# Transposes of the gated values, gate passes and convolution taps in other steps of a delta-rule attention loop

## What is computed

```python
qkvz = (x @ W_qkvz)                       # q, k, v, z
q, k, v = silu(causal 4-tap convolution of q, k, v)
def step(S, inp):                         # one token, one value head
    S = S * exp(g_t)
    delta = (v_t - k_t @ S) * beta_t
    S = S + outer(k_t, delta)
    return S, q_t @ S
gated = silu(z) * rms_norm(out) * norm_w
return gated @ W_out
```

## The kernel before, in words

| step | PE fill | ACT after copy | DVE after mask |
|---|---|---|---|
| 2 | inversion start g=1, last q passes | tanh v | conv K tap 3 |
| 3 | 7 Z0 | tap q | qk(0) |
| 4 | 7 Z0 | tanh k, gated(0) | qk(1) |
| 5 | 3 Z0, turn 0 | gated(1) | low(0) |
| 6 | 2 Z0, turn 1 | | low(1) |
| 7 | 5 Z0, product 0 | | add 0, conv Q tap 1 |
| 8 | product 1 | | add 1, conv Q tap 2 |
| 9 | product 2 | tanh q, tanh Z0 | add 2, conv Q tap 3 |
| 10 | product 3, 4 Z1 | | add 3 |
| 11 | 8 Z1 | | silu of Z0 |
| 12 | 4 Z1, transposes of k | squares of k | |
| 13 | 8 Z1 | | |

## Time and profile before

### The profile page before, as it was taken

How to read it: one execution, slowest core, us unless ns; L and a number is a source line. 1 busy time by engine, 2 the same in 40 slices (tenths; PEclk the granted TensorE clock), 3 DMA queues, 4 the chain that set the end, 5 groups by cost and what they waited for, 6 DMA issues and landing times. The chain is left out here.

```text
span 3966.3 us, 76921 instructions
## 1 busy us (share of the span) xinstructions
PE 3621.5 (91%) x29348; PEld 3031.0 (76%) x29348; DVE 2334.4 (59%) x4155; ACT 2062.8 (52%) x5168; POOL 2334.6 (59%) x2899
## 2 busy tenths in 40 slices
PE   5995699999999999999999999999999999997798
PEld 4884487878788878887878787878787888886587
DVE  4654466666666666666666666666666666663464
ACT  3432355555555555555555555555555555553243
POOL 2101567676767676767676767676766676763110
PEclk8997799999999999999999999999999999998899
DMA  4323100000000000000000000000000000000521
GB/s 159 104 32 69 50 23 23 22 24 23 24 22 23 23 23 23 23 22 23 23 24 22 24 22 23 23 24 23 23 23 23 22 23 23 22 26 24 176 54 33
DMA packets 142396, 140.47 MB, mean 35 GB/s; under 512 B 84176, under 2 KB 115152, under 8 KB 140880
## 3 DMA queue, kind: packets, MB, share of 16 engines
q1 hardware_dynamic: 136992, 120.16, 10.3%
q0 software_dynamic: 4464, 14.36, 1.0%
q10 hardware_dynamic: 576, 1.03, 0.1%
HBM read 109.11 MB, written 26.21 MB: 34 GB/s over the span
## 5 line engine op out<-in xcount | busy, mean ns | idle before, releaser
L1870 ACT ACTIVATE at_t<-at_inv 128x512 f16<-128x512 f32 x768 | 459.8, 599 | 591.9 <-PE at_inv L1679 591.9
L2054 DVE TENSOR_TENSOR at_pm<-at_prod,at_cst 128x512 f16<-128x512 f32 x768 | 529.4, 689 | 146.8 <-PE at_prod L1462 120.1
L1462 PE MATMUL at_proj<-x_hi,at_w_hi 128*128 128x512 f32 x1024 | 438.0, 428 | 15.6 <-POOL at_w_lo L2128 15.6
L1462 PE MATMUL at_proj<-x_lo,at_w_hi 128*128 128x512 f32 x1024 | 421.9, 412 | 0.0
L1462 PE MATMUL at_proj<-x_hi,at_w_lo 128*128 128x512 f32 x1024 | 416.5, 407 | 0.0
L1462 PE MATMUL at_prod<-at_t,at_nlhi 128*128 128x128 f16 x3584 | 367.6, 219 | 20.0 <-ACT at_t L1868 13.0
L2213 POOL TENSOR_TENSOR at_gt_lo<-at_cst,at_gates 128x512 fp32r<-128x512 f32 x256 | 262.1, 1045 | 115.2 <-PE at_misc L1462 115.1
L1462 PE MATMUL at_misc<-at_wo_hi,at_gt_hi 128*128 128x512 f32 x512 | 230.9, 451 | 94.5 <-DVE resid L2028 61.3
L1462 PE MATMUL at_proj<-at_w_hi,x_lo 128*128 128x256 f32 x1024 | 308.5, 301 | 0.0
L1462 PE MATMUL at_proj<-at_w_hi,x_hi 128*128 128x256 f32 x1024 | 297.9, 291 | 0.1
L1980 DVE SCALAR_TENSOR_TENSOR at_cv_v<-at_proj,at_cw,at_cv_v 128x511 f32<-128x511 f32 (+2 forms) x384 | 287.5, 749 | 16.3 <-ACT at_cv_v L1796 2.8
(11 more groups left out here) (291 smaller groups left out, 10829.0 us busy)
## 6 DMA issues: line engine op xcount, KB each, us to landing
at_gb<-decays SPq DMA_DIRECT2D x64, 512.0 KB, 3.6
at_e<-w_qkvz SPq DMA_DIRECT2D x32, 512.0 KB, 3.6
ffn_weights<-ffn_w SPq DMA_DIRECT2D x1, 11776.0 KB, 36.3
ffn_w<-ffn_weights POOLq DMA_DIRECT2D x4, 2688.0 KB, 23.8
at_gb<-w_qkvz SPq DMA_DIRECT2D x16, 512.0 KB, 3.6
at_gb<-w_out SPq DMA_DIRECT2D x16, 512.0 KB, 3.5
f_xnext<-x_in SPq DMA_DIRECT2D x4, 1024.0 KB, 5.3
f_xres<-x_res SPq DMA_DIRECT2D x4, 1024.0 KB, 5.3
```

The lines of the kernel that those rows point to most:

```text
L1462: return nc.tensor.matmul(out, lhsT, rhs, start=start, stop=stop)
L1870: own["a_t"].up(A(grown(t16[:, s % R].rearrange("p a t -> p (a t)"), s // R), grown(psT[s % R], s // R), ACT.Copy))
L2054: own["d_p"].up(V.tensor_tensor(pm[:, g].rearrange("p (c t) -> p c t", c=CH), psP[:].rearrange("p (c t) -> p c t", c=CH), mask.unsqueeze(1 ...
```

## The change

Gate passes are spread differently over the fill lists of steps 3 to 13, and those of steps 7 to 10 stand ahead of the output product of their step. Turn 0 moves from step 5 to step 4. On ACT, gated(0) moves from step 4 to step 3, tap q from 3 to 4, and tanh k from 4 to 6. On DVE, the qk products move up by one step, with a wait for ACT's squares added in front (L1872; they write the same tile), and taps 1 and 2 of q run in step 7 ahead of add 0, tap 3 in step 8 behind add 1. No arithmetic is added or taken away.

| step | PE fill | ACT after copy | DVE after mask |
|---|---|---|---|
| 2 | as before | as before | conv K tap 3, qk(0) |
| 3 | 5 Z0 | gated(0) | qk(1) |
| 4 | 5 Z0, turn 0 | tap q | |
| 5 | 5 Z0 | gated(1) | low(0) |
| 6 | turn 1, 2 Z0 | tanh k | low(1) |
| 7 | 4 Z0, product 0 | | conv Q taps 1 and 2, add 0 |
| 8 | 3 Z0, product 1 | | add 1, conv Q tap 3 |
| 9 | 4 Z1, product 2 | as before | add 2 |
| 10 | 4 Z1, product 3 | | add 3 |
| 11 | 6 Z1 | | as before |
| 12 | 3 Z1, transposes of k | as before | |
| 13 | 7 Z1 | | |

```diff
                 if has_delta:
-                    fill[3].append(gates_in(Z0_U, 0, 7))
-                    fill[4].append(gates_in(Z0_U, 7, 14))
-                    fill[5].append(gates_in(Z0_U, 14, 17))
-                    fill[6].append(gates_in(Z0_U, 17, 19))
-                    fill[7].append(gates_in(Z0_U, 19, 24))
+                    fill[3].append(gates_in(Z0_U, 0, 5))
+                    fill[4].append(gates_in(Z0_U, 5, 10))
+                    fill[5].append(gates_in(Z0_U, 10, 15))
                 if behind:
                     for h in range(R):
-                        fill[5 + h].append(lambda h=h: turn_gated(h, j - 1))
+                        fill[4 + 2 * h].append(lambda h=h: turn_gated(h, j - 1))
+                if has_delta:
+                    fill[6].append(gates_in(Z0_U, 15, 17))
+                    fill[7].append(gates_in(Z0_U, 17, 21))
+                    fill[8].append(gates_in(Z0_U, 21, 24))
+                    fill[9].append(gates_in(Z1_U, 0, 4))
+                    fill[10].append(gates_in(Z1_U, 4, 8))
+                if behind:
                     for c in range(WPROD):
                         fill[7 + c].append(lambda c=c: out_product(c, j - 1))
                 if has_delta:
-                    fill[10].append(gates_in(Z1_U, 0, 4))
-                    fill[11].append(gates_in(Z1_U, 4, 12))
-                    fill[12].append(gates_in(Z1_U, 12, 16))
-                    fill[13].append(gates_in(Z1_U, 16, 24))
+                    fill[11].append(gates_in(Z1_U, 8, 14))
+                    fill[12].append(gates_in(Z1_U, 14, 17))
+                    fill[13].append(gates_in(Z1_U, 17, 24))
...
-                if has_prep:
-                    steps[3].append(lambda: tap(Q_U))
-                    steps[4].append(lambda: tanh(K_U))
                 if behind:
                     for h in range(R):
-                        steps[4 + h].append(lambda h=h: gated(j - 1, h))
+                        steps[3 + 2 * h].append(lambda h=h: gated(j - 1, h))
+                if has_prep:
+                    steps[4].append(lambda: tap(Q_U))
+                    steps[6].append(lambda: tanh(K_U))
...
                 def qk(h):
                     wait(dve, "s_kq", j + 1)
+                    wait(dve, "a_sqo", R * j)
...
-                        steps[3 + h].append(lambda h=h: qk(h))
+                        steps[2 + h].append(lambda h=h: qk(h))
...
                 if behind:
                     for h in range(R):
                         steps[5 + h].append(lambda h=h: low(h, j - 1))
+                if has_prep:
+                    steps[7].append(lambda: conv(Q_U, (1, 2)))
+                if behind:
                     for c in range(WPROD):
                         steps[7 + c].append(lambda c=c: out_add(c, j - 1))
                 if has_prep:
-                    for i in range(3):
-                        steps[7 + i].append(lambda i=i: conv(Q_U, (i + 1,)))
+                    steps[8].append(lambda: conv(Q_U, (3,)))
```

## The result

The changed kernel takes 3971.11 us (median of 20 runs, 3967.64 to 3974.37), the kernel before in the same session 3964.34 (median of 20; one of its executions took 7055.8 us, all others 3958.97 to 3967.9). The ratio is 1.0018 (95% interval 1.0011 to 1.0025), about 7 us slower. The difference is clear of zero, and inside the 0.2% that the prediction called the same; the forecast was +4.2 us, a time of 3967.

What follows compares the result with a forecast made beforehand. PE was taken as the bottleneck, idling mainly before output products and turns. 62 full slots at +0.09 us less 1.35 in slot 63 gave +4.2 us: 3967.2 against the median of 3962.98, range 3950 to 3984.

Steps and rivals of the forecast that it cites:

- The bound and the step: Attention part: PE is the bottleneck; a step can't be shorter than P, mask, T, 1.41 us, into which seven passes just fit.
- the wait before Z1: Step 9: Z1's first pass waits for tap 3 behind add 1, a new PE wait of 1.16 us holding up product 2.
- Turn 0 one step earlier: Steps 4 to 7: turn 0 at 13.19 instead of 14.37 brings product 0 to 18.04 from 18.94, 0.90 us won.
- Passes and taps: Steps 3 to 13: redealt passes and moved taps bring new waits; with old waits gone, a slot changes by +0.09 us.
- add 0 is 0.31 late: Step 7 on DVE: taps 1 and 2 ahead of add 0 make it 0.31 us late; product 1 follows at 20.80.
- The cost of a product that needn't wait: Steps 9 and 10: 1.65 us taken for product 2 and 1.70 for product 3, between bounds of 1.64 and 1.74.
- Rival (a): Z1's first pass wakes 0.15 after its tap, products 2 and 3 take the full 1.74: +18 us, 3981; chance 0.25.
- Tanh of k, the step that failed: ACT step 6, behind gated(1) and copy(6): POOL's products of k start 2.0 us later, hidden by 0.1 us.
- stays within 0.1: Slot 0: it has no products, so its length was to change by no more than 0.1 us.
- rival (b): Tanh of k 1 us later than summed uncovers 0.9 us in some 15 weight-splitting slots: +14 us, 3981; chance 0.07.
- 62 x 0.09: Full slots: each of 62 grows by 0.09 us, old waits of 2.3 us giving way to new ones.
- rival (e): A 1.2 us wait takes PE to 1.2 GHz for the passes and product behind it: +136 us, 4103; chance 0.02.

Runs made afterwards that it cites:

- e10: The kernel of e6 with Z0 passes in steps 3 to 8 dealt 7, 3, 7, 1, 3, 3 instead of 5, 5, 5, 2, 4, 3; 3877.41 us.
- e1: The changed kernel with tap 3 of q moved ahead of add 1 on DVE in step 8; 3926.06 us, ratio 0.9900.
- e3: The changed kernel with Z1 beginning in step 10, eight passes ahead of product 3 and none in step 9; 3935.41 us, ratio 0.9923.
- e7: The kernel before with the turn part alone, tanh of k in step 6 as in the change; 3947.98 us, ratio 0.9956.
- e9: The kernel before with the turn part alone, tanh of k at the front of ACT's step 3; 3925.37 us, ratio 0.9903.
- e8: The changed kernel without the turn part, tanh of k back in step 4; 4036.70 us, ratio 1.0180.
- e5: The kernel of e1 with tanh of k moved from ACT's step 6 to the front of step 3; 3896.98 us, ratio 0.9827.
- e6: The kernel of e5 with one tap of q in each of steps 6, 7 and 8, ahead of low(1), add 0 and add 1; 3883.06 us.
- e4: The changed kernel with tanh of k back in step 4 where no unit is behind (slots -1 and 0); 3968.09 us, ratio 1.0006.
- e2: The changed kernel with tap 3 of q moved to step 9, behind mask(9) and ahead of add 2; 4006.22 us, ratio 1.0102.
- e11: The kernel of e1 with tanh of k moved from ACT's step 6 to step 5; 3904.80 us, ratio 0.9853.

## Why the prediction was right

**The bound and the step.** PE's list and its waits set the time, and a step is the longer of P-mask-T and PE's work: shown by the table above, by e10 (passes in steps 3 and 5 are free up to seven) and by e1 to e3, in which the time follows the wait before Z1 both ways.

**Turn 0 one step earlier.** Worth 0.91 us up to product 0, where the sum had 0.90. Alone it is worth 18 us with tanh of k where the change has it (e7), and 38 with tanh of k in step 3 (e9); taking it out of the changed kernel costs 66 (e8).

**Passes and taps.** The wait before Z1 is real and is the place against the change, as the sum had it: 1.16 behind P(9) + 0.20 by its arithmetic, 0.97 us in the profile's way of counting idle time, the first pass at 13.01 for 13.00. Its cause is the order on DVE, tap 3 behind add 1: with the two exchanged, 45 us go (e1), and with POOL's part mended 74 (e5). That add 0 is 0.31 late because of the two taps holds too, at 14 us for 19 (e6). Without the turn part, passes and taps as changed are 71 us slower than before (e8). The parts don't simply add up: 18 won by the turn part alone (e7) and 71 lost by the rest alone (e8) would make 53 slower, and together they are 7 slower. One reason shows in the rows: with seven passes ahead of it turn 0 comes 0.95 earlier than before (2.52 behind P(3) in e7, for 3.47) and product 0 by 0.67, while with five passes it comes 1.41 earlier (2.29 in the changed kernel, for 3.70 in e8) and product 0 by 1.14. The other is the wait for the scaled k, which e7's shorter slots lay bare: e9, with only 0.4 us of it left, is 23 us faster than e7.

**The cost of a product that needn't wait.** Estimated at 1.65; product 2 to P(10) is 1.64, product 3 to P(11) 1.68 (1.70 was taken for it). Rival (a), that both cost the 1.74 of one that waited, falls, as does its late wake-up (0.06, not 0.15).

**Tanh of k, the step that failed.** The prediction said of slot 0 that it "stays within 0.1", and rival (b) put POOL's lateness only into the slots that split weights. In the full slots it was right: POOL starts 2.0 us later, and its 2.08 us of idle time ahead of the split are used up to the last tenth:

```profile
2025.17 1.29 POOL L2169 TENSOR_TENSOR at_th<-at_th,at_cv_k 128x512 f32<-128x512 f32 x1 [1.99 <-ACT at_th L1813]
...
2039.80 0.61 POOL L2134 CAST at_w_hi<-at_gb 128x512 fp32r<-128x512 f32 x1
```

The split starts with no idle time of POOL ahead of it, and PE's wait for the scaled k is 0.34, as small as before. But slot 0 is short (39 us from transposes to transposes, not 50), and POOL has less room there. By itself the new place makes POOL's products of k 2.2 us later in slot 0 (from its first P: 9.34 us, in e4 7.10); PE then waits 2.03 us for the scaled k, and the clock falls behind that wait. In the trace against e4's this is 2.2 us in slot 0 and 1.6 in slot 1, the second only where the clock does fall: in e1 slot 1 stays at the length of the others. DVE's lists add 0.7 in slot 0. These are the terms that the prediction put at "within 0.1".

The total is right in part by luck. The sum left out these 4 to 5 us and had 62 x 0.09 = 5.6 for the full slots where the trace shows 3.2 (slots that split weights grew by nothing), so the two errors go against each other, and the total came out less than 3 us low. What was not luck is that a full slot stays as long as it was, and why: the old waits go, and the wait before Z1 takes their place.

**The clock, rival (e).** Where it was looked for, before Z1, it does not happen: not at 0.97 us, nor at 1.56 us in e2, where the granted clock is 1.00 throughout. Nor behind the 1.26 of turn 1 in e8. It does happen at the transposes of the scaled k: in 9 of 15 cases at 1.2 to 1.4 us in e1 and in 8 of 15 at 1.2 in e7; with 0.8 to 1.0 us at the same place, in e11 and e3, in none. In slot 0 it happens behind 2.03 us in the changed kernel, and not behind 2.03 in e1 or 2.49 in e7. The Trainium skill, "TensorE: Matmul & The Clock Gate", section "A second HAM failure mode: psum-queue depth-cycling", says that frequent short idles between groups of matmuls can make the clock swing; e1 and e7 agree at one place in the slot, and e2 shows that a longer idle elsewhere need not. What decides it, the place, the work around it or the moment at which the wait falls, wasn't tried.

## What to carry to other kernels

A task put ahead of another in an in-order list is only free if its own wait is over by then: before moving PE's passes ahead of a product, follow the bank they write back to the engine that frees it, and see what stands ahead of the freeing operation there. If two engines wait for each other through a chain, exchanging two operations on the less busy engine can be worth more than the whole rearrangement (one moved line: 45 us). Sum each kind of slot by itself, the first and the last too: an operation that is hidden in the full slot may be bare in a short one, and slack used up to the last tenth turns the next gain elsewhere into a wait.

## What the runs showed of the hardware

The granted clock can fall behind a single wait of PE of 1.2 to 1.4 us, and it does so in about half of the cases at one and the same place (9 of 15 in e1, 8 of 15 in e7). A fall costs about 1.5 us in the slot behind (50.05 instead of 48.55 us in e1, 50.5 instead of 49.0 in e7). A longer wait doesn't make it certain: 2.03 us (e1) and 2.49 us (e7) at that place left the clock at 1.00, as did 1.56 us before Z1 in all slots of e2.

With nothing but T between a product and the next P, a product of six matmuls of 512 columns took 1.74 to 1.76 us from its start to that P where PE had waited before it, and 1.63 to 1.70 us behind four or eight gate passes without a wait; the difference is in the distance from its first matmul to the second (0.34 us, against 0.23 to 0.29). Behind three passes without an idle time in the profile it took 1.75 too (product 1 in e6 and e10), and why wasn't tried.
